# Where alpha's transposes stand in the TensorE queue of a graph attention layer: behind nine steps of the sum instead of eight

## The reference

```python
def gat_layer(x, W, a_s, a_d, edges):              # 8 heads, 768 features each
    h = (x @ W).reshape(n, H, C)
    e = leaky_relu((h * a_s).sum(-1)[src] + (h * a_d).sum(-1)[dst], 0.2)
    p = exp(e - segment_max(e, dst)[dst])
    alpha = p / segment_sum(p, dst)[dst]
    return segment_sum(h[src] * alpha[:, :, None], dst).reshape(n, H * C)
# x = x + gat_layer(gat_layer -> elu, W2 with one head); afterwards the feed-forward layer
```

## Time and profile before

| | |
|---|---|
| Median of the runs | 1407.78 us |
| Profiled execution | 1407.49 us |
| Its span | 1405.7 us |
| TensorE busy | 1310.6 us, 93% |
| VectorE busy | 1004.6 us, 71% |
| ScalarE busy | 627.4 us, 45% |
| GpSimd busy | 217.0 us, 15% |
| Looped heads of layer 0, at the transposes | 97.78 to 286.10 us |
| Looped heads of layer 1, at the transposes | 415.88 to 605.75 us |

### The profile page before, as it was taken

How to read it: one execution, slowest core, us unless ns; L and a number is a source line. 1 busy time by engine, 2 the same in 40 slices (tenths; PEclk the granted TensorE clock), 3 DMA queues, 4 the chain that set the end, 5 groups by cost and what they waited for, 6 DMA issues and landing times.

```text
span 1405.7 us, 21373 instructions
## 1 busy us (share of the span) xinstructions
PE 1310.6 (93%) x7833; PEld 1149.2 (82%) x7833; DVE 1004.6 (71%) x1677; ACT 627.4 (45%) x795; POOL 217.0 (15%) x160
## 2 busy tenths in 40 slices
PE   5799999997899999997898999999999999999986
PEld 4499999974689999975777898898889888988875
DVE  7888888877797888875856765666566556656565
ACT  2256665644355666553434433433343334333431
POOL 0033444431024344431000000000000000002000
PEclk9999999998999999998999999999999999999988
DMA  9466556653256555653334454445444544543520
GB/s 346 147 202 198 164 164 180 213 134 93 91 196 199 180 164 164 192 160 113 113 111 152 163 198 170 149 166 199 158 149 177 195 149 149 188 177 134 177 69 23
DMA packets 103718, 227.32 MB, mean 162 GB/s; under 512 B 16688, under 2 KB 34672, under 8 KB 103684
## 3 DMA queue, kind: packets, MB, share of 16 engines
q1 hardware_dynamic: 72780, 192.43, 39.1%
q10 hardware_dynamic: 20968, 31.78, 7.7%
q0 software_dynamic: 9936, 2.66, 1.9%
HBM read 216.56 MB, written 10.29 MB: 161 GB/s over the span
## 4 chain that ended last, share of the span: by engine, by line
PE 61%; DVE 24%; issue 8%; ACT 4%; DMA 1%; DVEq 1%; ACTq 0%; SPq 0%
PE bank L418 59%; DVE w_lo L1181 6%; DVE hid_lo L1181 2%; DVE h_lo L1181 2%; DVE neg_b L1325 1%; ACT w_hi L892 1%; DVE scores_b L1276 1%; DVE stats L1219 1%; DVE scores_b L1278 1%; ACT z_b L960 1%; DMA w_in<-L_gnn_W 1%; DVE scores_b L1187 1%; PE bank L457 1%; DVE same L1299 1%; PE bank L514 1%
## 5 line engine op out<-in xcount | busy, mean ns | idle before, releaser
L1181 DVE TENSOR_TENSOR w_lo<-w_in,w_hi 128x2304 fp32r<-128x2304 f32 (+4 forms) x162 | 396.4, 2477 | 57.9 <-ACT w_hi L892 57.7
L892 ACT ACTIVATE w_hi<-w_in 128x2304 fp32r<-128x2304 f32 (+4 forms) x162 | 328.2, 2062 | 224.3 <-PE bank L418 197.2
L418 PE MATMUL bank<-w_hi,xT_hi 128*128 128x384 f32 (+3 forms) x942 | 324.1, 344 | 6.9 <-DVE xT_lo L1181 4.5
L418 PE MATMUL bank<-w_lo,xT_hi 128*128 128x384 f32 (+3 forms) x942 | 309.7, 341 | 0.0
L418 PE MATMUL bank<-w_hi,hid_hi 128*128 128x512 f32 (+2 forms) x858 | 293.9, 343 | 5.8 <-DVE hid_lo L1181 3.5
L418 PE MATMUL bank<-w_lo,hid_hi 128*128 128x512 f32 (+2 forms) x858 | 271.7, 337 | 0.0
L418 PE MATMUL bank<-w_hi,xT_lo 128*128 128x384 f32 (+3 forms) x942 | 248.0, 342 | 0.0
L418 PE MATMUL bank<-w_hi,hid_lo 128*128 128x512 f32 (+2 forms) x858 | 224.6, 339 | 0.0
L418 PEld LDWEIGHTS bank<-w_hi,xT_hi 128*128 128x128 f32 (+1 forms) x942 | 179.2, 190 | 36.4 <-issue 8.3
L418 PEld LDWEIGHTS bank<-w_hi,hid_hi 128*128 128x128 f32 (+1 forms) x858 | 161.7, 188 | 42.2 <-issue 5.3
L418 PEld LDWEIGHTS bank<-w_lo,xT_hi 128*128 128x128 f32 (+1 forms) x942 | 178.7, 190 | 13.7
(11 more groups left out here) (225 smaller groups left out, 1575.1 us busy)
## 6 DMA issues: line engine op xcount, KB each, us to landing
w_in<-L_gnn_W_rel SPq DMA_DIRECT2D x68, 1152.0 KB, 5.6
w_in<-L_gnn_W SPq DMA_DIRECT2D x66, 1152.0 KB, 5.8
table<-zrow SPq DMA_DIRECT2D x1, 9216.0 KB, 36.0
scores_b<-table ACTq DMA_DIRECT2D x34, 256.0 KB, 3.0
a_bc<-L_gnn_a_src ACTq DMA_DIRECT2D x18, 384.0 KB, 3.7
a_bc<-L_gnn_a_dst ACTq DMA_DIRECT2D x18, 384.0 KB, 5.0
key_row<-key_rows ACTq DMA_DIRECT2D x16, 256.0 KB, 5.5
w_in<-ffn_out SPq DMA_DIRECT2D x4, 864.0 KB, 7.2
```

The lines of the kernel that those rows point to most:

```text
L418: return pe.matmul(out, lhsT, rhs, start=start, stop=stop, **kw)
L892: act.activation(out, ps, func, **kw).then_inc(mark, 1)
L1181: return dve.tensor_tensor(out, a, b, op)
```

## The change

In the looped heads the transposes of alpha are put behind nine steps of the preceding head's sum; three steps follow them, not four. The instructions are the same, in another order on TensorE. The code is one for both layers.

```diff
                     up(h, h * 2 + n0)
                     down(h - 1, h * 2 + (n0 + 1), 0, 3)
                     spread(h + 9 * layer)
-                    down(h - 1, h * 2 + (n0 + 1), 3, 8)
+                    down(h - 1, h * 2 + (n0 + 1), 3, 9)
                     turn(h + 9 * layer)
-                    down(h - 1, h * 2 + (n0 + 1), 8, M * K)
+                    down(h - 1, h * 2 + (n0 + 1), 9, M * K)
                     parts_kept(h + 9 * layer)
                     attend(h)
```

## The result

The changed kernel took 1393.02 us (median of 4 runs, 1392.79 to 1394.66), the kernel before 1407.32 (4 runs, 1406.12 to 1408.96). The ratio is 0.9904, with a 95% interval of 0.9888 to 0.9920: faster by 14.3 us. The forecast was 1394.7, in a range of 1392.3 to 1399.5.

What follows compares the result with a forecast made beforehand. A loop of VectorE's chain, alpha's transposes, four steps and the attention product was taken to bound the looped heads. Gains of 5.8 (layer 0) and 7.3 us (layer 1), 13.1 in all, gave 1394.7 us, range 1392.3 to 1399.5.

Steps and rivals of the forecast that it cites:

- The loop: Looped heads: VectorE's chain, alpha's transposes, four steps, attention product, which restarts VectorE; a step moved ahead gains up to 1.05 us.
- The gap is idle + 0.16: TensorE at alpha's transposes: real loss per head is the idle shown plus 0.16 us, 0.83 where 0.67 showed.
- Nothing late next: Work the moved step had covered (alpha's copy and low part, z's minimum), weight loads, GpSimd, clock: cost nothing.
- Slack of the low part at attend: Alpha's low part on VectorE would be ready 0.86 us before the attention product, about 0.65 in layer 1.
- The copy: ScalarE's copy of transposed alpha would end at 130.73, still before VectorE's low part starts at 131.54; cost nothing.
- its terms for the two layers: Gain from filling TensorE's waits for alpha in seven looped heads each: layer 0 5.8 us, layer 1 7.3 us.
- spread's pitch unchanged: Scalar-column product, line 502, starting 0.46 us after its predecessor instead of 0.35: expected to stay so.
- The 0.34 that was to stay at the longest gap: Layer 1 head at 511 us: gap 1.39 us exceeds the 1.05 step, so 0.34 stays as a wait.
- C: Rival: the wait only moves to the scalar-column product of line 502; no gain, 1407.8 us; chance 4%.
- D: Rival: alpha's low part comes late for the attention product, 14 x 0.9 = 12.6 us, giving 1420.4; chance 3%.
- B: Rival: VectorE's chain lengthens in most heads by GpSimd overlaps, 0.27 us each; 1398.5 us; chance 14%.
- E: Rival: GpSimd blocks VectorE for whole instructions, up to 1.56 us in every head; 1416.5 us; chance 2%.

Runs made afterwards that it cites:

- first repetition: The changed kernel run again without further edits, beside the kernel before on the same chip: 1392.46 us, ratio 0.9896.
- two repetitions: The changed kernel run twice more without further edits: 1392.46 us (ratio 0.9896 to the kernel before) and 1392.55 us (ratio 0.9903).

## Why the prediction was right, and where its sizes were off

**The loop** held, from both sides. A step behind the transposes costs 1.02 us per head (one step the other way, in layer 0 alone or with the wait filled), a further one ahead of them costs nothing (ten steps), and shortening VectorE's part instead removes the same wait.

**The gap is idle + 0.16.** The pitch at the transposes fell from 1.18 to 0.35 where 0.67 of idle was shown; in layer 0 all seven heads now have 0.35 or 0.36.

**Nothing late next.** Slack of the low part at attend 0.79 us (0.86 forecast), in layer 1 0.63 (0.65); idle ahead of the first minimum of z 0.25 (0.24); granted clock 1.00. The copy ended at 129.74 (129.14 + 0.60), not 130.73. That time was reckoned without the gain of the heads ahead of this one, by which the whole head lies 0.93 sooner (spread's transposes at 121.65, not 122.58); behind its own transposes the copy ends after 1.24 us (128.50 to 129.74), with 1.29 forecast.

**The sum was 1.6 us short of the traces' difference,** 13.1 against 14.69, and its terms for the two layers were too small. Layer 0 brought 6.41, not 5.8. When alpha is ready ahead of its transposes, the next step follows them by 0.35 and not 0.41, 7 x 0.06 = 0.4; most of the remaining 0.2 is spread, whose pitch in one head was 0.65 and is 0.45 at most now. I had called spread's pitch unchanged. Layer 1 brought 7.86, not 7.3. The 0.34 that was to stay at the longest gap did not. In the kernel before, a small VectorE instruction of that head took 0.51 us beside a GpSimd scatter, and 0.17 to 0.19 in the other six heads:

```profile
509.59 0.51 DVE L1184 TENSOR_SCALAR small<-small 128x2 f32<-128x2 f32 x1
```
```profile
508.90 1.72 POOL L377 DMA_INDIRECT table<-value,row_i  x1 [4.80 <-DMA table<-value,row_i]
```

No head of the changed kernel's profile has this. The first repetition has it once (532.38, 0.52), and there TensorE waits 0.19 at a pitch of 0.71. So the wait "in one or two heads" that was forecast depends on how the two engines' phases fall, and its absence here is luck. Besides, 0.65 us came behind the loops and 0.23 went between the layers; the sum had no term for either, and both are smaller than the 1.5 and 2.3 us by which repetitions differ in these stretches. Medians of the two repetitions were 12.9 and 13.7 us below before, so the time alone does not tell 13.1 from 14.3.

**The rivals.** C fell: spread did not become later. D fell here, and came true with two steps more (a wait in each head) but not with one (none), as a slack of 0.8 us lets one expect. B and E fell: from z to alpha VectorE needs 21.21 us, 21.28 before, and in the middle heads of layer 1 21.42 to 21.51, as before. On E's rule, the exclusive lock of the Trainium skill ("SBUF — State Buffer", "SBUF: two separate sides"): the sum over the heads left no room for blocking by whole instructions of 1.56 us, and what the rows show beside a GpSimd scatter is 0.27 and 0.32 to 0.34 for the instruction at 509.59.

## What to carry to other kernels

Where an in-order engine waits for a chain that its own later work releases, look for the loop, and count which work stands in it. A block of work that is moved ahead of the wait gains the smaller of its own pitch and the gap, and then stops; the next thing that it covered sets how far one can go, so read that slack first. A wait of TensorE can cost more than its length, through the clock: price such a wait with both.

## What the hardware showed that was not expected

With idle times of up to 1.8 us once per head, the granted clock stayed at 1.00 (layer 0 with seven steps ahead). With 1.91 to 2.3 us, five of seven heads fell to a granted clock of 0.77 over the 7.3 us behind the wait, a loss of 1.5 us each on top of it, and two with waits of 1.96 and 2.28 did not. With six matmuls on zeros in the wait no head fell. The Trainium skill ("TensorE: Matmul & The Clock Gate", "What's actually happening") says that the clock is gated by how busy the engine has been of late, and the fill's effect agrees with that.

A VectorE instruction of 128x2 elements in layer 1 took 0.17 to 0.20 us, and 0.51 or 0.52 in eight heads of five traces. In each of the eight a GpSimd scatter had started 0.55 to 0.75 us before it. In no other head of the thirteen traces did one start within those bounds, and where it had started 0.50 or 0.84 us before, the instruction took its 0.17 to 0.19. The two waits of 2.28 and 2.29 us with seven steps, and the longest wait of the kernel before, 1.23, are in such heads. Why that moment counts was not tried.
